# Group normalisation in front of a recurrent, attention and feed-forward kernel: statistics read from PSUM, normalising moved to GpSimd, the products of one image placed between the turns of the next

## What is computed

```python
def _gn(v, G=32, eps=1e-5):
    B_, H_, W_, C_ = v.shape
    g = v.reshape(B_, H_, W_, G, C_ // G)
    m = jnp.mean(g, axis=(1, 2, 4), keepdims=True)
    s = jnp.var(g, axis=(1, 2, 4), keepdims=True)
    return ((g - m) / jnp.sqrt(s + eps)).reshape(v.shape)
```

## Time and profile before

| | us |
|---|---|
| median of 3 runs | 6811.03 |
| lowest, highest | 6809.58, 6813.49 |
| the profiled execution | 6810.61 |
| its span, first to last instruction | 6808.7 |

### The profile page before, as it was taken

One profiled execution on the slowest core, in us unless ns is written; L12 is line 12 of the kernel. 1 busy time (PEld: TensorE's weight loads), 2 busy tenths in 40 slices (PEclk: granted clock), 3 DMA queues, 4 the chain that ended last, 5 costly groups with the idle time before them and its releaser, 6 DMA issues. The chain is left out here.

```text
span 6808.7 us, 240684 instructions
## 1 busy us (share of the span) xinstructions
PE 6191.8 (91%) x100325; PEld 3736.2 (55%) x100560; DVE 3093.8 (45%) x8331; ACT 3215.1 (47%) x9215; POOL 1857.0 (27%) x2255
## 2 busy tenths in 40 slices
PE   4499999997888887989999999979999999999999
PEld 3499888995666665983444444433333333333333
DVE  7677777775777765434666666610000000000000
ACT  4366555564666664334555555523333333333333
POOL 1000000004767762005777777710000000000000
PEclk6699999998999999898999999989999999999999
DMA  6631112125766661014555555411111211211111
GB/s 265 257 115 67 69 50 75 58 102 178 218 216 205 206 201 38 0 33 127 154 155 154 155 157 154 127 54 44 55 44 43 56 43 43 56 43 47 52 44 42
DMA packets 785139, 715.35 MB, mean 105 GB/s; under 512 B 68336, under 2 KB 662256, under 8 KB 781040
## 3 DMA queue, kind: packets, MB, share of 16 engines
q1 hardware_dynamic: 769712, 599.13, 28.7%
q0 software_dynamic: 14400, 101.45, 3.7%
HBM read 390.60 MB, written 307.89 MB: 103 GB/s over the span
## 5 line engine op out<-in xcount | busy, mean ns | idle before, releaser
L2096 PE MATMUL f_junk<-f_idle 128*32 128x384 bf16 x24736 | 1566.7, 323 | 2.4 <-issue 2.4
L2139 ACT ACTIVATE f_y<-f_acc 128x16 f32<-128x16 f32 x4096 | 753.7, 184 | 1553.8 <-PE f_acc L2107 1553.8
L2107 PEld LDWEIGHTS f_acc<-f_y,f_vT 128*32 128x32 f32 x32768 | 649.2, 108 | 1412.1 <-ACT f_y L2139 1401.1
L2107 PE MATMUL f_acc<-f_y,f_vT 128*32 128x16 f32 x32768 | 1049.7, 193 | 58.0 <-issue 9.5
L2054 DVE TENSOR_TENSOR f_sum<-f_turned,f_t 128x512 f32<-128x512 f32 x128 | 88.5, 691 | 1762.9 <-PE f_turned L2089 1762.9
L1826 DVE TENSOR_REDUCE o_m<-o_bank_l 128x8 f32<-128x512 f32 x512 | 325.6, 678 | 382.0 <-remote 372.8
L2096 PEld LDWEIGHTS f_junk<-f_idle 128*32 128x32 bf16 x24736 | 447.0, 96 | 4.5 <-issue 4.2
L399 ACT ACTIVATE l_gate<-l_pf,l_bf 128x256 f32<-128x256 f32 (+12 forms) x768 | 273.4, 407 | 229.0 <-PE l_pf L374 228.4
L336 POOL DMA_DIRECT2D hidden<-l_h x48 | 36.2, 754 | 1256.9 <-DVE l_hsum L453 1191.9
L916 ACT ACTIVATE a_p<-a_s 128x512 f32<-128x512 f32 x512 | 264.3, 602 | 194.0 <-PE a_s L807 194.0
L365 PE MATMUL l_pf<-l_x,l_wf 128*128 128x256 f32 (+12 forms) x1536 | 317.9, 330 | 36.7 <-DMA l_x<-skew 36.7
(11 more groups left out here) (253 smaller groups left out, 12939.2 us busy)
## 6 DMA issues: line engine op xcount, KB each, us to landing
a_hid<-hidden SPq DMA_DIRECT2D x112, 520.0 KB, 4.6
hidden<-l_h POOLq DMA_DIRECT2D x48, 1040.0 KB, 6.4
skew<-gn_skew POOLq DMA_DIRECT2D x8, 6144.0 KB, 23.8
l_x<-skew SPq DMA_DIRECT2D x48, 1024.0 KB, 5.2
vals<-a_v SPq DMA_DIRECT2D x128, 272.0 KB, 3.0
o_v<-vals SPq DMA_DIRECT2D x128, 272.0 KB, 3.5
gn_x<-in_x SPq DMA_DIRECT2D x16, 2048.0 KB, 12.4
a_xin<-in_x SPq DMA_DIRECT2D x128, 256.0 KB, 4.4
```

Of the source, the lines that this page charges most:

```text
L2096: nc.tensor.matmul(junk[rows, :], idle[:, 0:QUAD], idle[:, :], start=True, stop=True)
L2107: mm = nc.tensor.matmul(acc[k % 2][rows, t, :], vT[:, rows], before, start=False, stop=True, skip_group_check=True)
L2139: nc.scalar.activation(y[q][:, u, :], acc[u // RC % 2][:, u % RC, :], ACT.Sigmoid).then_inc(s_y, 1)
```

## The change

In `group_norm_phase` alone:

- The statistics read the PSUM bank (`sums`), and ScalarE copies a bank after its statistics (`s_stats`) instead of before. There are 6 banks for 4, and two buffers for `stats`, `gmean` and `rstd`.
- GpSimd normalises: one `tensor_scalar` per image that subtracts the group mean and multiplies by `rstd`, in place in `D`. The shift is gone.
- The product of the means of image k - 1 stands after the third bank of image k, that of the spreads after the fifth. On VectorE `centre(k - 1)` follows the second statistics of image k, `variance(k - 1)` the fourth.
- The loops are written out. The two small stores are gone; VectorE clears `D[0]`, GpSimd `D[1]`.

```diff
--- before.py
+++ after.py
@@ -64,33 +64,34 @@
     with ExitStack() as ctx:
         m = Memory(nc, ctx)
+        TB = 6
         xin = [m.sb(f"gn_x{s}", [P, NT, C]) for s in range(SETS)]
         D = [m.sb(f"gn_skew{q}", [P, STEPS * G]) for q in range(2)]
         ident = m.sb("gn_ident", [P, P])
         avg = m.sb("gn_avg", [P, P])
-        stats = m.sb("gn_stats", [P, 8, 6])
+        stats = [m.sb(f"gn_stats{k}", [P, 8, 6]) for k in range(2)]
 ...
-        gmean = m.sb("gn_gmean", [P, 1])
+        gmean = [m.sb(f"gn_gmean{k}", [P, 1]) for k in range(2)]
 ...
-        rstd = m.sb("gn_rstd", [P, 1])
+        rstd = [m.sb(f"gn_rstd{k}", [P, 1]) for k in range(2)]
-        shift = m.sb("gn_shift", [P, 1])
-        turned = [m.ps(f"gn_turned{k}", [P, 4, P]) for k in range(4)]
+        turned = [m.ps(f"gn_turned{k}", [P, 4, P]) for k in range(TB)]
         group = m.ps("gn_group", [P, 512])
         s_const = sems.sem("gn_const")
-        s_avg = sems.sem("gn_avg")
         s_clear = sems.sem("gn_clear")
         s_load = [sems.sem(f"gn_load{s}") for s in range(SETS)]
         s_turned = sems.sem("gn_turned")
         s_copied = sems.sem("gn_copied")
+        s_stats = sems.sem("gn_stats")
 ...
-        s_rstd = sems.sem("gn_rstd")
+        s_pool = sems.sem("gn_pool")
         s_store = [sems.sem(f"gn_store{q}") for q in range(2)]
-        VS = 9 + 6
+        VS = 5
+        NK = SETS * LANES
 ...
@@ -104,112 +105,128 @@
         @block.sync
         def _(sp):
-            def load(q, s, it):
-                sp.dma_start(xin[s][:, :, :], x[8 * s + 2 * it + q].rearrange("(p n) c -> p n c", n=NT)
-                             ).then_inc(s_load[s], 16)
-
-            with sp.Fori(0, LANES // 2) as it:
-                for q in range(2):
-                    for s in range(SETS):
-
-                        sp.wait_ge(s_turned, 32 * it + 16 * q + 8 * s + 8)
-                        load(q, s, it)
+            for k in range(NK):
+                lane, s = k // SETS, k % SETS
+                if k >= SETS:
+                    sp.wait_ge(s_turned, 8 * (k - 1))
+                sp.dma_start(xin[s][:, :, :], x[8 * s + lane].rearrange("(p n) c -> p n c", n=NT)).then_inc(s_load[s], 16)
         @block.gpsimd
         def _(pool):
             make_identity(pool, ident, s_const)
 ...
+            pool.memset(minus_half[:, :], -0.5).then_inc(s_const, 1)
+            pool.memset(D[1][:, :], 0.0).then_inc(s_const, 1)
+            pool.wait_ge(s_const, 6)
+            for k in range(NK):
+                lane, s = k // SETS, k % SETS
+                pool.wait_ge(s_vec, VS * (k + 1))
+                pool.tensor_tensor(rstd[k % 2][:, :], veps[:, :], minus_half[:, :], ALU.pow).then_inc(s_pool, 1)
+                pool.wait_ge(s_pool, 2 * k + 1)
+                pool.wait_ge(s_copied, 8 * (k + 1))
+                pool.tensor_scalar(image(lane % 2, s), image(lane % 2, s), gmean[k % 2][:, 0:1], rstd[k % 2][:, 0:1],
+                                   ALU.subtract, ALU.mult).then_inc(s_pool, 1)
+                if s == SETS - 1:
+                    pool.wait_ge(s_pool, 2 * k + 2)
+                    pool.dma_start(skew[lane], D[lane % 2][:, :]).then_inc(s_store[lane % 2], 16)
             for q in range(2):
-                pool.memset(D[q][:, :], 0.0).then_inc(s_clear, 1)
-
-            pool.wait_ge(s_clear, 2)
-            for q in range(2):
-                pool.dma_start(skew[q, 0:1, 0:1], D[q][0:1, 0:1]).then_inc(s_store[q], 16)
-            pool.memset(minus_half[:, :], -0.5).then_inc(s_avg, 1)
-            pool.wait_ge(s_avg, 4)
-            with pool.Fori(0, LANES // 2) as it:
-                for q in range(2):
-                    for s in range(SETS):
-                        k = 4 * it + 2 * q + s
-
-                        pool.wait_ge(s_vec, VS * k + 13)
-                        pool.tensor_tensor(rstd[:, :], veps[:, :], minus_half[:, :], ALU.pow).then_inc(s_rstd, 1)
-                    pool.wait_ge(s_vec, VS * (4 * it + 2 * q + 2))
-                    pool.dma_start(skew[2 * it + q], D[q][:, :]).then_inc(s_store[q], 16)
-            for q in range(2):
-                pool.wait_ge(s_store[q], 16 * (LANES // 2 + 1))
+                pool.wait_ge(s_store[q], 16 * (LANES // 2))
         @block.tensor
         def _(pe):
-            pe.sem_inc(s_turned, 16)
-            pe.wait_ge(s_const, 2)
-            pe.wait_ge(s_avg, 3)
-            with pe.Fori(0, LANES // 2) as it:
-                for q in range(2):
-                    for s in range(SETS):
-                        k = 4 * it + 2 * q + s
-                        pe.wait_ge(s_load[s], 16 * (2 * it + q + 1))
-                        for g in range(8):
-
-                            pe.wait_ge(s_copied, 8 * k + g + 1)
-                            for n in range(4):
-                                last = nc.tensor.transpose(turned[g % 4][:, n, :], xin[s][:, 4 * g + n, :], ident[:, :])
-                            last.then_inc(s_turned, 1)
-                        pe.wait_ge(s_vec, VS * k + 9)
-                        nc.tensor.matmul(group[:, 0:1], avg[:, :], mv[:, 0:1], start=True, stop=True).then_inc(s_group, 1)
-                        pe.wait_ge(s_vec, VS * k + 12)
-                        nc.tensor.matmul(group[:, 0:1], avg[:, :], spread[:, :], start=True, stop=True).then_inc(s_group, 1)
+            pe.wait_ge(s_const, 5)
+            def mean_of_groups(k):
+                pe.wait_ge(s_vec, VS * k + 1)
+                nc.tensor.matmul(group[:, 0:1], avg[:, :], mv[:, 0:1], start=True, stop=True).then_inc(s_group, 1)
+            def spread_of_groups(k):
+                pe.wait_ge(s_vec, VS * k + 4)
+                nc.tensor.matmul(group[:, 0:1], avg[:, :], spread[:, :], start=True, stop=True).then_inc(s_group, 1)
+            for k in range(NK):
+                lane, s = k // SETS, k % SETS
+                pe.wait_ge(s_load[s], 16 * (lane + 1))
+                for g in range(8):
+                    n = 8 * k + g
+                    if n >= TB:
+                        pe.wait_ge(s_copied, n - TB + 1)
+                    for j in range(4):
+                        last = nc.tensor.transpose(turned[n % TB][:, j, :], xin[s][:, 4 * g + j, :], ident[:, :])
+                    last.then_inc(s_turned, 1)
+                    if k and g == 2:
+                        mean_of_groups(k - 1)
+                    if k and g == 4:
+                        spread_of_groups(k - 1)
+            mean_of_groups(NK - 1)
+            spread_of_groups(NK - 1)
         @block.scalar
         def _(act):
-            act.sem_inc(s_copied, 4)
-            act.wait_ge(s_clear, 2)
-            with act.Fori(0, LANES // 2) as it:
-                for q in range(2):
-                    act.wait_ge(s_store[q], 16 * it + 16)
-                    for s in range(SETS):
-                        k = 4 * it + 2 * q + s
-                        for g in range(8):
-                            act.wait_ge(s_turned, 16 + 8 * k + g + 1)
-                            nc.scalar.copy(chunk(q, s, g), turned[g % 4][:, :, :].rearrange("c n (i h) -> c n i h", h=2)).then_inc(s_copied, 1)
+            for k in range(NK):
+                lane, s = k // SETS, k % SETS
+                if lane == 0:
+                    act.wait_ge(s_clear, 1)
+                elif lane == 1:
+                    act.wait_ge(s_const, 7)
+                elif s == 0:
+                    act.wait_ge(s_store[lane % 2], 16 * (lane // 2))
+                for g in range(8):
+                    act.wait_ge(s_stats, 8 * k + g + 1)
+                    nc.scalar.copy(chunk(lane % 2, s, g), turned[(8 * k + g) % TB][:, :, :].rearrange("c n (i h) -> c n i h", h=2)
+                                   ).then_inc(s_copied, 1)
         @block.vector
         def _(dve):
-            with dve.Fori(0, LANES // 2) as it:
-                for q in range(2):
-                    for s in range(SETS):
-                        k = 4 * it + 2 * q + s
-                        for g in range(8):
-                            dve.wait_ge(s_copied, 4 + 8 * k + g + 1)
-                            nc.vector.bn_stats(stats[:, g, :], strided(chunk(q, s, g)[:, 0:1, 0:1, 0:1], [[G, 4], [G + 1, G], [G * NT, 2]])).then_inc(s_vec, 1)
-                        dve.drain()
-                        nc.vector.bn_aggr(mv[:, :], stats[:, :, :]).then_inc(s_vec, 1)
-                        dve.wait_ge(s_group, 2 * k + 1)
-                        nc.vector.tensor_copy(gmean[:, :], group[:, 0:1]).then_inc(s_vec, 1)
-                        dve.wait_ge(s_vec, VS * k + 10)
-
-                        nc.vector.tensor_tensor(dev[:, :], mv[:, 0:1], gmean[:, :], ALU.subtract).then_inc(s_vec, 1)
-                        dve.wait_ge(s_vec, VS * k + 11)
-                        nc.vector.scalar_tensor_tensor(out=spread[:, :], in0=dev[:, :], scalar=dev[:, 0:1], in1=mv[:, 1:2],
-                                                       op0=ALU.mult, op1=ALU.add).then_inc(s_vec, 1)
```

(39 more changed lines are left out.)

10 lines of the change are left out of this document (5 added, 5 removed).

## The result

| | us |
|---|---|
| before, median of 4 | 6810.31 |
| with the change, median of 4 (6893.97 to 6905.63) | 6898.43 |
| ratio, 95% interval | 1.0133 [1.0118, 1.0148] |
| span of the profiled execution | 6903.9 |

The change costs 88 us where 66 were to be saved. The next phase begins at 388.5 us instead of 300.3, which is the whole difference of the medians. (The two profiled spans differ by 95.2 us: the profiled execution was the longest of the four, 7.2 above their median.)

A forecast was written before the change was run, and what follows sets the result against it. VectorE was taken to bound group normalisation at 15.86 us per image. First store at 39.4, three rounds of 53.2, then 17.3 and 16.2 end at 232.5 instead of 298.9, 66.4 us less: 6744 us, range 6726 to 6786.

The forecast's parts named there:

- The step that failed: GpSimd's strided tensor_scalar normalising one image: 1.0 ns per column plus 1.0 for the stride, 8 us, ends 4.1 and 12.
- The upper end of 10.2 us: GpSimd's normalising, bounded from above by two-input operations at 1.04 to 1.27 us per 512 columns: 8.3 to 10.2 us.
- The estimate of 9.9 us: GpSimd's normalising by the skill's 2.9 cycles per element for inner steps over 8 bytes; the sum would give 6757 us.
- Rival 4: GpSimd's normalising passes 15.2 us, 3.7 ns per column, making the kernel slower; at 18 us, 6849 us. Chance 0.05.
- The rest of the sum: Group normalisation: first store at 39.4 us, three rounds of 53.2, 17.3 for lane 7, landing 16.2 later at 232.5.
- what is late next: Two skew buffers: copies wait for an earlier store, the next load meets another store; 53.2 us per two lanes.
- Rival 3: VectorE's two-input dev and spread wait for GpSimd's long operation to end; about 240 us, 6752 us. Chance 0.08.
- the hold: VectorE's dev, with two SBUF inputs, stopped by GpSimd's long operation; rounds would slip by 2 to 3 us.
- The sign that the prediction gave for rival 3: On the timeline, the small VectorE operations start exactly at the ends of GpSimd's.
- the statistics at 0.65 us: VectorE's statistics read from PSUM, contiguous, bounded by 0.60 and 0.96 us: eight cost 5.2 us instead of 7.7.
- the early start: Clearing split between VectorE and GpSimd: first copy at about 12.3 us instead of 27.37, first store at 39.4 instead of 61.13.
- Rival 1: Loads fall between stores, 48.6 us per two lanes, or GpSimd takes 4.1 us, round 49.3; 6728 us. Chance 0.14.

The follow-up runs named there:

- e2_one_input: The changed kernel with VectorE's dev and spread formed from one tensor input each instead of two in SBUF; 6895.51 us, ratio 1.0125.
- e3_vector: The changed kernel with one-input dev and spread and the normalising back on VectorE, behind the sixth statistics of the next image; 6756.11 us, ratio 0.9925.
- e7_own_products: e3_vector with the products, centring, variance and normalising of a lane's second image right behind its own turns and statistics; 6737.90 us, ratio 0.9891.
- e8_three_buffers: e3_vector with three skew buffers instead of two, GpSimd clearing the third as well; 6734.18 us, ratio 0.9891.

## Why the prediction was wrong

- **The step that failed** is the price of GpSimd's tensor_scalar, "I take 1.0 + 1.0 ns: 8 us per image, ends 4.1 and 12". It took 20.6 us, 5.0 ns per column, beyond the upper end. Both parts of it were too small. The base of 1.0 ns came from affine_select, the nearest one-input row; a contiguous tensor_scalar takes 3.5 ns. Of the stride it had 1.0 ns, where 1.6 were measured. The upper end of 10.2 us from two-input rows is what failed as a bound: the two-input operation with a broadcast scalar (7.0 us contiguous) is cheaper than the one-input tensor_scalar (14.1). The estimate of 9.9 us that the prediction took from the Trainium skill (GPSIMD Engine Reference, Performance pitfalls for Q7 kernels) was as far off.
- Rival 4, slower than before beyond 3.7 ns per column, is what came, with its mechanism: GpSimd back to back, each image pushed by the one before. Its formula, 22 + 16 x (W + 0.65) + 16.9, gives 379 us for W = 20.6; the phase ended at 388.5, with the first power 1.9 us later and 0.9 us around each lane's store that the formula leaves out. It had a chance of 0.05 because it stood at "twice the dearest row of GpSimd per column", and rows of other operations were taken as a limit for this one.
- **The rest of the sum** had the right path and was too low. With a GpSimd operation of 9 us and no hold the time is 6764.6; the prediction's sum for that size (41.4 + 3 x 54.2 + 19.3 + 16.2 = 239.5) is 6751 us, 14 too low: its rounds were 57.5 to 59.3 us. With VectorE's own operation they were 55.8 us where the same terms give 50: the load beside a store took 19.8 us instead of 15 and the store 21.7 instead of 20.5. So the wait named under "what is late next" was there, in pairs of stores as described, and undersized by 3 to 6 us per round. At 9 us on GpSimd the measured time lies inside the range that was given, so this error alone would not have undone the forecast.
- Rival 3, the hold, is real, and 0.08 was too little for it. The trace before even showed it. In 122 of its 128 executions line 1875 starts in the last 0.16 to 0.34 us of a GpSimd tensor_tensor on 512 columns (line 1568) and ends 0.53 to 0.56 us after that one: 0.73 us long where 0.18 were to go, 0.87 where 0.32 were. It was stopped to the end each time, and the median of 732 ns hid that. Three others start within a power of four columns (line 1571), with 0.9 us to go, and take 0.68 us: that one holds nothing up. One of the 122 (start us, us, engine, operation):

```profile
3144.61 1.05 POOL L1568 TENSOR_TENSOR o_z<-o_t,o_mv 128x512 f32<-128x512 f32 x1
...
3145.33 0.87 DVE L1875 TENSOR_TENSOR o_att<-o_pvs,o_rden 128x512 f32<-128x512 f32 x1
```

In the change as made the hold cost nothing (e2_one_input), at 9 us 8.5 us. Its length is not the whole reason: a tensor_scalar lets `dev` go 3.4 us before its end and the 2.2 us that follow fit in, a copy holds it to the end and they don't. The sign that the prediction gave for rival 3, small operations that start exactly at the ends of GpSimd's, does not come in the change.

- Right: the statistics at 0.65 us (683 ns each, two of them in 1.29), the early start (rstd of image 0 at 24 us, foreseen at 22; the first copy at 15.8 for 12.3, since ScalarE's table load also waits for the first statistics, at 14.51), VectorE's work (without the held `dev` its 308.9 us busy are 102.7, 115 less than before; 120 were foreseen), VectorE, TensorE and ScalarE below the bound, and the LSTM unchanged: over 100 us from some 11.6 us behind its start VectorE is busy 73.3 us in 370 instructions against 73.5 in 371 before. The unrolled code and the six banks were not tested by themselves; e3_vector and e7_own_products have both, so what they cost leaves the kernel 53 and 71 us quicker than before.
- Rival 1, no collision of load and store, did not come. e7_own_products and e8_three_buffers come near its time, 6738 and 6734 us for its 6728, but not by its mechanism: their loads meet the stores and take 19.0 and 17.0 us at the median, more than the 12.4 before.
